# A convolution and window-attention kernel: strip loads move ahead of strip stores in SyncE's queue, and the copies of a wrapped strip are issued one strip later

## What is computed

```python
def _L0_conv_ref(x, ...):                       # a bottleneck with a residual
    h = relu(bn(conv1x1(x, w1)))                # 128 -> 64
    h = relu(bn(conv3x3(h, w2, groups=32)))
    h = bn(conv1x1(h, w3))                      # 64 -> 128
    return relu(h + x)

def _L1_conv_ref(x, ...):                       # a Swin block, 7 x 7 windows, shift 3
    y = roll(layernorm(x), (-3, -3), axis=(1, 2))
    win = windows(y)                            # 64 windows of 49 tokens an image
    q, k, v = heads(win @ qkv_w.T)              # 8 heads of 16
    attn = softmax(q @ k.T * scale + bias + mask)
    out = windows_back((attn @ v) @ proj_w.T + proj_b)
    x = x + roll(out, (3, 3), axis=(1, 2))
    z = layernorm(x)
    return x + gelu(z @ fc1_w.T + fc1_b) @ fc2_w.T + fc2_b
```

## Time and profile before

| | |
|---|---|
| median of 3 runs | 4834.04 us (4832.89 to 4839.28) |
| the profiled execution | 4831.1 us, of which the span on the core is 4829.0 us |
| first layer and set-up | up to about 760 us |
| strips | about 4040 us for 256 |
| PE busy | 4439.0 us, 92% of the span |
| ACT, DVE, POOL busy | 71%, 67%, 46% |
| mean granted clock of PE | 0.973 of full |

### The profile page before, as it was taken

How to read it: one execution, slowest core, us unless ns; L and a number is a source line. 1 busy time by engine, 2 the same in 40 slices (tenths; PEclk the granted TensorE clock), 3 DMA queues, 4 the chain that set the end, 5 groups by cost and what they waited for, 6 DMA issues and landing times.

```text
span 4829.0 us, 192181 instructions
## 1 busy us (share of the span) xinstructions
PE 4439.0 (92%) x71190; PEld 3280.4 (68%) x71190; DVE 3214.6 (67%) x7717; ACT 3444.2 (71%) x5644; POOL 2213.1 (46%) x3242
## 2 busy tenths in 40 slices
PE   8999996999999999999999999999999999999998
PEld 5666665666667666667666666666666666677665
DVE  4343435777777777777777777777777777777775
ACT  3444445777787777777777777777777777787776
POOL 4444433444444444444444444444444444444443
PEclk9999998999999999999999999999999999999999
DMA  4445441011001001000001001010010010000000
GB/s 141 148 146 158 147 137 42 27 28 28 27 27 27 26 27 28 26 27 27 27 27 28 27 27 27 27 27 27 27 28 27 27 28 27 27 27 27 26 27 24
DMA packets 298330, 218.64 MB, mean 45 GB/s; under 512 B 43377, under 2 KB 245518, under 8 KB 298190
## 3 DMA queue, kind: packets, MB, share of 16 engines
q1 hardware_dynamic: 294632, 215.41, 15.3%
q10 hardware_dynamic: 3558, 1.07, 0.1%
HBM read 110.73 MB, written 111.94 MB: 46 GB/s over the span
## 4 chain that ended last, share of the span: by engine, by line
issue 51%; POOL 30%; PE 15%; POOLq 2%; DVE 1%; ACT 0%; DMA 0%; DVEq 0%; ACTq 0%
POOL lnp L1145 15%; POOL sc L1222 12%; PE bank L501 6%; PE bank L514 4%; POOL res L1209 2%; PE bank L479 2%; PE bank L470 2%; POOL lnp L1197 1%; POOLq L1219 0%; PE bank L658 0%; POOLq L104 0%; POOLq L111 0%; PE bank L577 0%; POOLq L1195 0%; DVE sc L1051 0%
## 5 line engine op out<-in xcount | busy, mean ns | idle before, releaser
L1222 POOL TENSOR_TENSOR sc<-sc,mx 128x784 f32<-128x784 f32 x512 | 780.1, 1524 | 973.8 <-DVE mx L1057 973.8
L1209 POOL TENSOR_TENSOR res<-x,projb 98x512 f32<-98x512 f32 x256 | 327.5, 1279 | 1072.3 <-DVE x L1093 1072.3
L850 ACT ACTIVATE g<-bank,fc1b 128x392 f32<-128x392 f32 x1024 | 560.2, 592 | 244.7 <-PE bank L651 244.6
L658 PE MATMUL bank<-g,fc_sb 128*128 128x392 f32 x2048 | 716.7, 493 | 0.1
L914 DVE BATCH_NORM_STATS2 st<-x 98x6 f32<-98x128 f32 x2048 | 446.5, 281 | 260.7 <-DMA x<-x_scratch 252.0
L1076 DVE SCALAR_TENSOR_TENSOR xn<-x,lnp 98x128 f32<-98x128 f32 x1024 | 292.8, 348 | 446.7 <-POOL lnp L1145 445.8
L600 PEld LDWEIGHTS bank<-ident_sb,sc 128*113 128x113 f32 x4096 | 496.3, 177 | 106.7 <-DVE shared L1027 103.9
L633 PE MATMUL bank<-wproj,ot 128*98 128x128 f32 x2048 | 310.7, 299 | 269.2 <-DVE ot L1064 269.2
L1051 DVE TENSOR_TENSOR sc<-bank,shared 128x392 f32<-128x392 f32 x1024 | 528.3, 558 | 34.0 <-PE bank L587 33.8
L600 PE MATMUL bank<-ident_sb,sc 128*113 128x128 f32 x4096 | 541.6, 275 | 0.0
L577 PE MATMUL bank<-xt,wqkv 128*128 128x392 f32 x1024 | 480.0, 552 | 39.2 <-ACT xt L825 9.9
(11 more groups left out here) (105 smaller groups left out, 8451.2 us busy)
## 6 DMA issues: line engine op xcount, KB each, us to landing
x<-x_scratch SPq DMA_DIRECT2D x768, 49.0 KB
out_x<-y SPq DMA_DIRECT2D x672, 49.0 KB
xc_even<-in_x SPq DMA_DIRECT2D x128, 196.0 KB
shared<-in_x SPq DMA_DIRECT2D x128, 196.0 KB
x_scratch<-xc_even SPq DMA_DIRECT2D x128, 196.0 KB
x_scratch<-shared SPq DMA_DIRECT2D x128, 196.0 KB
x<-x_scratch SPq DMA_DIRECT2D x256, 38.5 KB
out_x<-y SPq DMA_DIRECT2D x224, 38.5 KB
```

The lines of the kernel that those rows point to most:

```text
L658: mm = nc.tensor.matmul(RC[:, 0:ST], fc2[:, c, :], g[:, c], start=c == 0, stop=c == HC - 1)
L850: nc.scalar.activation(g[:, j], ring[:, 0:ST], ACT.Gelu, bias=fc1b[:, j:j + 1]).then_inc(out_, 1)
L1222: P.tensor_tensor(out=s_r, in0=s_r, in1=m_r.to_broadcast([128, 2 * HEADS, N]), op=ALU.subtract).then_inc(sub_done, 1)
```

## The change

It touches only SP's program. LEAD goes from 5 to 6, so each load is issued one place earlier: the queue reads load n, store n-6, load n+1, store n-5. The two copies of a wrapped strip, with the wait ahead of them, leave `store_strip` and become `unwrap(img)`, which stands behind the load and the store of the next strip. Load 6 and store 0 are taken out of the first turn and written ahead of the loop; each turn of the loop begins with strip 1 and ends with strip 0 of the next image and `unwrap`. The counts waited for are the same, and so is every DMA.

```diff
-LEAD = 5
+LEAD = 6
...
                     for c, j0, nj in columns(p):
                         sp.dma_start(block(dst, img, row, c, nj),
                                      y[WIN * j0:WIN * (j0 + nj), u, p, :]).then_inc(y_out[u], 16)
-                if wraps:
-                    sp.wait_ge(y_out[u], 16 * MOVES * (STRIPS // 2) * (img + 1))
-                    below = WIN - SHIFT
-                    sp.dma_start(out[img, H - below:H], wrap_dram[img, 0:below]).then_inc(wrapped, 16)
-                    sp.dma_start(out[img, 0:SHIFT], wrap_dram[img, below:WIN]).then_inc(wrapped, 16)
+
+            def unwrap(img):
+                u = (STRIPS - 1) % 2
+                sp.wait_ge(y_out[u], 16 * MOVES * (STRIPS // 2) * (img + 1))
+                below = WIN - SHIFT
+                sp.dma_start(out[img, H - below:H], wrap_dram[img, 0:below]).then_inc(wrapped, 16)
+                sp.dma_start(out[img, 0:SHIFT], wrap_dram[img, below:WIN]).then_inc(wrapped, 16)
...
             for s in range(2, LEAD):
                 load_strip(0, s, s % 2)
+            load_strip(0, LEAD, LEAD % 2)
+            store_strip(0, 0, 0)
             with sp.Fori(0, B - 1) as img:
-                for s in range(STRIPS):
+                for s in range(1, STRIPS):
                     if s + LEAD < STRIPS:
                         load_strip(img, s + LEAD, (s + LEAD) % 2)
                     else:
                         load_strip(img + 1, s + LEAD - STRIPS, (s + LEAD) % 2)
                     store_strip(img, s, s % 2)
-            for s in range(STRIPS):
+                load_strip(img + 1, LEAD, LEAD % 2)
+                store_strip(img + 1, 0, 0)
+                unwrap(img)
+            for s in range(1, STRIPS):
                 if s + LEAD < STRIPS:
                     load_strip(B - 1, s + LEAD, (s + LEAD) % 2)
                 store_strip(B - 1, s, s % 2)
+            unwrap(B - 1)
```

## The result

The changed kernel takes 4635.1 us (median of 4 runs, 4629.75 to 4640.65) against 4834.6 before (4 runs, one more than in the table above): a ratio of 0.959, with a 95% interval of 0.957 to 0.960. The forecast was 4641 us, and its range 4612 to 4664. The profiled execution took 4629.75 us, its span 4627.6.

The account below looks back on a forecast made before the run. The prediction took the ring through `ot`, delayed by late loads, to bound the kernel. Savings of 105, 71 and 17 us made 193, so 4834.04 - 193.0 = 4641 us; forecast 4625 to 4662 (0.78), range 4612 to 4664 (0.82).

Parts of the forecast that it names:

- The ring: Chain `ot`, PE's last product, `x2`, `res1` and factors on POOL, `xn`, scores, maxima, statistics, `z`, `ot`; claimed without slack.
- P to `ot`: Time from the start of POOL's second subtraction (P) to the start of `ot`; forecast at 2.38 us in every strip.
- Ordinary strips: The 186 strips away from wraps: wait for the load gone, 0.09 us gained each on the mean, 17 us in all.
- 0.6 of the 0.69 us: Apparent gain of 0.69 us per ordinary strip; `z`, held by POOL's subtraction, leaves a mean of 0.09.
- The strip behind the wrapped store, 105 us: Load no longer behind the wait and copies: interval falls from 18.35 to 14.96 us, 3.39 saved 31 times.
- The strip after it, 71 us: Second strip behind a wrap, where PE's clock had fallen: from 17.25 to 14.96 us, 2.29 saved 31 times.
- What the change adds, 0 us: Later stores, moved copies and reordered prologue on SP: priced at 0, bounds 0 to 1 us a wrapped strip.
- the 2 us in hand: SP's room at a wrapped strip: load, store and copies take 12.8 of 14.96 us, so the next load is on time.
- The rival of a weaker lock (4601): `ot` held only by ACT's `rsum`, not by the lock on `z`: further 0.16 us a strip, 4601 us; chance 0.06.
- The lock: POOL's SBUF subtraction blocks DVE's two-input `z`, which takes 1.84 us instead of 1.12, so `ot` starts no earlier than P + 2.38.
- The slower rival: SP's queue becomes the bound if issues cost more without pauses; about 5,800 us at 1.945 us an issue; chance 0.03.
- my threshold of 3.05: Load lateness in us that brings the time back to 4834: 1.7 in hand, 0.6 hidden, 0.75 to eat the gain.

Follow-up runs that it names:

- the factor experiments: Changed kernel with POOL's factors for `xn` and `z` worked out apart: 4619.8 us; the same without POOL's wait for `xn` before `z`'s factors: 4605.0 us.
- the run with 7 issues: Changed kernel with two of the five DMAs of each load split in two, same bytes: 4637.3 us.
- the run with 8 issues: Changed kernel with three of the five DMAs of each load split in two, same bytes: 4878.2 us.
- 8 issues with two images a turn: Changed kernel with three of each load's five DMAs split in two and SP's loop taking two images a turn: 4800.2 us.

## Why the prediction was right, step by step

- **What bounds the kernel.** Right. The ring from `ot` over PE's last product, `x2`, POOL and `xn` set the strip, and what a load's lateness added to P to `ot` came off the time. "No link in it has slack" was true, but said too little: the factor experiments show PE's own order only 0.1 us behind.
- **Ordinary strips.** Right in mechanism and size: the wait is gone, `z` is at 1.84, P to `ot` at 2.38. The floor is 14.95 where I had 14.96. That 0.6 of the 0.69 us is worth nothing could be read from the early load in the trace of before, and the run with 7 issues confirms it from the other side: put the wait back, and no time is lost.
- **The strip behind the wrapped store, 105 us.** The size is right: these strips take 15.0 us or less. I wrote that the load now stands ahead of the wait and the copies, and that reads as if both edits were needed. The order alone takes the time from 4829.2 to 4637.4 us, all of the gain. The later copies alone take it to 4776.3, 53 us, and add nothing to the order.
- **The strip after it, 71 us.** Right: full clock throughout, and the runs show that PE's idle time was the cause.
- **What the change adds, 0 us.** Right, with the 2 us in hand as worked out.
- **The sum.** 193 us forecast, 195.7 measured between strips 2 and 251, 199.5 between the medians. The forecast time is 6 us above the measured one, within the scatter of the runs (11 us). 2.7 of the 6 lie in the strips; the rest lies outside them, where nothing was changed.
- **The rival of a weaker lock (4601).** Didn't happen. The lock binds as in the sample.
- **The slower rival.** It didn't happen, and its arithmetic held where it applied: 1.7 us in hand and 0.6 free. A load 2.8 us later gave a wait of 1.08 and 0.45 us a strip, where mine gives 1.1 and 0.5. But the run with 8 issues was slower than the kernel before, at a lateness of 2.8 that is below my threshold of 3.05: the rival's sum gives about 4770 us for it (4641 + 256 x 0.5), and it took 4878.2. The step that failed was to price an issue by its time on SP alone. It also has a size in code, and past a certain one each turn of the loop pays some 2.4 us more than the 0.7 it took.

## What to carry to other kernels

A queue that one engine serves in order is judged at its fullest place: find which work in it gates the others (loads), put it ahead of what nobody waits for (stores), and count the room left at the fullest strip, with the size of the loop's code as a room of its own (8 issues a load cost 78 us more in one loop than in another). Before a stall is booked as gain, look in the same trace for an instance without it: here a strip near the end showed that an instruction behind the stall would grow by as much as the stall shrank. And count a long idle of PE twice, once for itself and once for the slow clock behind it.

## What the runs showed of the hardware

- PE's granted clock behind idle time is no fixed step: at 2.7 to 3.0 us of idle time it fell in 23 of 30 cases and stayed in 7, in one kernel and at the same place; at 3.3 to 4.2 us it fell in all 74 cases of three kernels (before, 8 issues, 8 issues with two images a turn), and at the 0.4 to 1.1 us of ordinary strips it never did.
- POOL's subtraction of 784 elements a partition holds DVE's normalizing instruction until 0.14 us after its end (1.05 us instead of 0.34), and until 0.08 us after it in the form with a single tensor input (0.99 instead of 0.34). DVE's statistics are not held, and a power instruction of 1.07 us on 4 elements holds none of them.
- SP's issue costs about 1.0 us for each DMA of a strip whether it covers 98 rows or 49: 5 take 4.97, 7 take 6.9, 8 take 7.8 us. Behind the loop, where the same 5 are written out, they take 4.3.
- A turn of SP's loop costs 0.7 us with 82 DMAs in the body, and 2.9 to 3.3 us with 106, when 5 packets of code are fetched in each turn, one of them in the gap. With 98 DMAs it is at most 1.0 and nothing is fetched at the turns.
